# Matmuls ordered by PSUM bank, layer two moved by one chunk, and a new order on VectorE, in a one-core graph layer

## The reference

```
h = relu(layernorm(x))
e = concat(h[src], h[dst], edge_attr)        # 400000 x 96
v = relu(e @ W1 + b1) @ W2 + b2              # 96 -> 64 -> 32
out = x + maximum(segment_max(v, dst), h)
```

## Time and profile before

| | us |
|---|---|
| median of 3 runs | 3184.88 |
| lowest and highest run | 3180.12 and 3187.65 |
| span of the profiled execution | 4798.8 |

### The profile page before, as it was taken

The page is one execution under the profiler, slowest core; times in us unless marked ns, Lnnn a source line. Parts: engine busy times, 40 slices in busy tenths (PEclk is TensorE's granted clock), DMA queues, the critical chain, the costliest instruction groups (busy, mean ns, idle before and its releaser), DMA issues.

```text
span 4798.8 us, 56874 instructions
## 1 busy us (share of the span) xinstructions
PE 3796.5 (79%) x19778; PEld 2547.3 (53%) x19778; DVE 2178.1 (45%) x2474; ACT 2192.4 (46%) x2555; POOL 2386.6 (50%) x2523
## 2 busy tenths in 40 slices
PE   5858788778878877877887788778877887778787
PEld 3536455555555545555555555555555555555465
DVE  4211554445444444544444455444444454445356
ACT  2214454445444444544444445444544454445355
POOL 6653455555455455455545555555455555554310
PEclk8979888888778888888887888888888888888798
DMA  8700222222222222222222222222222222222112
GB/s 255 279 10 25 70 80 88 92 85 61 57 68 63 56 66 69 56 61 68 68 55 63 68 65 61 60 69 68 56 63 68 69 61 56 68 68 68 46 55 56
DMA packets 200553, 350.32 MB, mean 73 GB/s; under 512 B 73791, under 2 KB 124251, under 8 KB 200117
## 3 DMA queue, kind: packets, MB, share of 16 engines
q1 hardware_dynamic: 116638, 303.65, 18.4%
q0 software_dynamic: 80448, 41.33, 6.2%
q10 hardware_dynamic: 3332, 4.01, 0.3%
HBM read 240.36 MB, written 119.78 MB: 75 GB/s over the span
## 4 chain that ended last, share of the span: by engine, by line
PE 60%; issue 19%; another core or an unknown queue 10%; DVE 8%; ACT 2%; DMA 0%; DVEq 0%; ACTq 0%; SPq 0%
PE ps_rows L938 38%; PE ps_layers L968 8%; PE ps_layers L963 5%; DVE onehot L1250 3%; PE ps_layers L918 2%; PE ps_layers L953 2%; PE ps_layers L912 2%; DVE max_t L1318 2%; PE ps_layers L957 2%; PE ps_layers L1006 1%; DVE src_t L1285 1%; DVE rows_in L1323 1%; ACT onehot L852 0%; DVE dst_t L1305 0%
## 5 line engine op out<-in xcount | busy, mean ns | idle before, releaser
L664 POOL DMA_INDIRECT src_in<-h_dram,src_ix x2269 | 2147.7, 947 | 1951.5 <-PE ps_rows L938 976.5
L938 PE MATMUL ps_rows<-onehot,table 128*128 128x512 f32 x9898 | 2553.2, 418 | 109.0 <-issue 89.3
L938 PEld LDWEIGHTS ps_rows<-onehot,table 128*128 128x128 f32 x9898 | 1986.6, 203 | 728.8 <-issue 292.8
L852 ACT ACTIVATE onehot<-distance 128x1024 fp32r<-128x1024 bf16 x909 | 905.0, 1049 | 855.0 <-PE ps_rows L938 607.3
L847 ACT ACTIVATE distance<-picks,below_column 128x1024 bf16<-128x1024 int16 x909 | 985.1, 1139 | 0.7 <-DMA picks<-picks_dram 0.7
L838 ACT ACTIVATE hid<-ps_layers,b_col 128x512 f32<-128x512 f32 (+1 forms) x404 | 241.6, 680 | 1407.9 <-remote 912.0
L1300 DVE STREAM_TRANSPOSE ps_layers<-rows_in 128x512 f32<-128x512 f32 x202 | 133.3, 706 | 1561.3 <-ACT hid L838 1561.2
L968 PE MATMUL ps_layers<-picked_rows,w_src 128*64 128x128 f32 x1552 | 399.9, 390 | 550.1 <-issue 545.7
L1250 DVE SCALAR_TENSOR_TENSOR onehot<-picks,column,ps_layers 128x1024 fp32r<-128x1024 int16 x404 | 499.8, 1258 | 310.2 <-PE ps_rows L938 164.7
L968 PEld LDWEIGHTS ps_layers<-picked_rows,w_src 128*64 128x64 f32 x1552 | 188.8, 180 | 784.9 <-issue 782.2
L1318 DVE TENSOR_TENSOR_SCAN max_t<-mask_in,max_t,ps_layers 128x512 f32<-128x512 bf16 x196 | 249.0, 1271 | 337.2 <-remote 331.4
(11 more groups left out here) (145 smaller groups left out, 1283.1 us busy)
## 6 DMA issues: line engine op xcount, KB each, us to landing
picks<-picks_dram SPq DMA_DIRECT2D x101, 512.0 KB
first_rows<-hid SPq DMA_DIRECT2D x100, 500.0 KB
rows_in<-in_edge_attr_dram SPq DMA_DIRECT2D x96, 512.0 KB
rows_in<-first_rows SPq DMA_DIRECT2D x96, 512.0 KB
run_max<-rows_in SPq DMA_DIRECT2D x96, 512.0 KB
src_in<-h_dram,src_ix POOLq DMA_INDIRECT x2269
mask_in<-mask_dram SPq DMA_DIRECT2D x96, 256.0 KB
h_dram<-h_sb ACTq DMA_DIRECT2D x4, 392.0 KB, 5.9
```

The costliest lines, as they stand in the source:

```text
L664: pool.indirect_dma_start(out=src_in[:, slot, g, r, :], out_offset=None, in_=rows[:, :], in_offset=bass.IndirectOffsetOnAxis(ap=src_ix[:, ...
L852: nc.scalar.activation(onehot[:, RING_AT[c] + BY_DVE[c] + k, :, :].rearrange("p g w -> p (g w)"), distance[:, k, :], ACT.Relu, bias=1.0, s ...
L938: mm = nc.tensor.matmul(ps_rows[g][side][:, 0:WIDE], table[:, i * SIDES + side, part, :], onehot[:, RING_AT[c] + t, g, :], start=(i + part ...
```

## The change

1. `look_up` goes bank by bank. Before, each tile was multiplied into all four banks in turn; now a chunk's tiles all go into bank (side 1, g 0), then (1, 1), (0, 0) and (0, 1). The number of matmuls stays. A counter `banks_summed` tells that a bank is complete in the last chunk; the three tiles of the last chunk are counted together at its end, and in the others `tiles_used` rises at the end of a bank. Chunk 0 waits for the masks of each bank by itself.
2. `mask_rows` starts on each bank when that bank is summed.
3. Layer two stands behind chunk 1 of the look-up instead of behind chunk 0.
4. VectorE's order in a pair becomes: one-hot 0, `mask_rows`, `turn_edges`, `turn_src`, then a wait for the ReLUs of pair j, one-hot 2, `fill_dst`, `find_side`, one-hot 3, `find_max`.
5. Layer one is cut into four functions that TensorE still runs one after the other.

```diff
+BANKS = [(1, 0), (1, 1), (0, 0), (0, 1)]
...
-            def look_up(j, slot, c):
-                if c == 0:
-                    wait(pe, rows_masked, j * MASKS)
-                if BY_DVE[c]:
+            def look_up_bank(j, c, n):
+                side, g = BANKS[n]
+                if c == 0 and (not isinstance(j, int) or j > 0):
+                    if side:
+                        pe.wait_ge(second_side, j * 2 - 1 + g)
+                    else:
+                        pe.wait_ge(rows_masked, j * MASKS - 1 + g)
+                if n == 0 and BY_DVE[c]:
                     pe.wait_ge(onehot_made, j * DVE_ALL + (DVE_AT[c] + 1))
                 for t in range(CHUNK[c]):
...
+                    for part in range(parts):
+                        mm = nc.tensor.matmul(ps_rows[g][side][:, 0:WIDE], table[:, i * SIDES + side, part, :],
+                                              onehot[:, RING_AT[c] + t, g, :],
+                                              start=(i + part == 0), stop=(i == last_tile and part == parts - 1))
+                if c == CHUNKS - 1:
+                    if n < len(BANKS) - 1:
+                        mm.then_inc(banks_summed, 1)
+                    else:
+                        mm.then_inc(tiles_used, CHUNK[c])
+                elif n >= len(BANKS) - CHUNK[c]:
                     mm.then_inc(tiles_used, 1)
...
-                look_up(j + 2, slot, 0)
+                    look_up(j + 2, 0)
+                look_up(j + 2, 1)
                 if mini:
                     layer_two_mini(j, ps_v)
                 else:
                     layer_two(j)
-                for c in range(1, CHUNKS):
-                    look_up(j + 2, slot, c)
+                for c in range(2, CHUNKS):
+                    look_up(j + 2, c)
...
             def mask_rows(j, slot):
                 wait(dve, hid_summed, j * A - A)
-                dve.wait_ge(tiles_used, j * TILES + WIDE_TILES)
                 for g in range(2):
+                    dve.wait_ge(banks_summed, j * (len(BANKS) - 1) + (g + 1))
...
                 turn_edges(j + 1, 1 - slot, of_next * D + D)
+                turn_src(j + 1, (k + 1) % (2 * AHEAD), turn + (k + 1) // (2 * AHEAD))
+                dve.wait_ge(hid_made, j * A + A)
+                dve.sem_inc(layer_passed, 1)
+                one_hot(j + 2, slot, 2)
                 fill_dst(j + 1, 1 - slot, of_next * D + D, of_next * D + D, j + 1)
-                one_hot(j + 2, slot, 2)
+                find_side(j + 2, slot)
+                one_hot(j + 2, slot, 3)
                 find_max(j, slot, stored)
-                one_hot(j + 2, slot, 3)
-                find_side(j + 2, slot)
-                turn_src(j + 1, (k + 1) % (2 * AHEAD), turn + (k + 1) // (2 * AHEAD))
```

More of the change, by code:

```diff
@@ L928, in look_up @@
                     pe.wait_ge(onehot_made, j * DVE_ALL + (DVE_AT[c] + 1))
                 for t in range(CHUNK[c]):
-                    if t == BY_DVE[c]:
+                    i = CHUNK_AT[c] + t
+                    if n == 0 and t == BY_DVE[c]:
                         pe.wait_ge(act_onehot_made, j * ACT_ALL + (ACT_AT[c] + BY_ACT[c]))
[L932 to L940, removed]
+                    if side and i >= WIDE_TILES:
+                        continue
@@ L941, in look_up, with layer_edges @@
                     mm.then_inc(tiles_used, 1)
-            def layer_one(j, slot, ahead=True, short=False):
+            def look_up(j, c):
+                for n in range(len(BANKS)):
+                    look_up_bank(j, c, n)
+            def layer_edges(j, slot):
                 wait(pe, max_scanned, j * 2)
-                pe.wait_ge(onehot_made, j * DVE_ALL + (2 * DVE_ALL + 1 if ahead else (PAIRS - j) * DVE_ALL))
-                pe.wait_ge(side_found, j + 2 if ahead else PAIRS)
-                pe.wait_ge(dst_filled, j * 2 + 2 if ahead else PAIRS * 2)
+                pe.wait_ge(onehot_made, j * DVE_ALL + (2 * DVE_ALL + 1))
+                pe.wait_ge(side_found, j + 2)
+                pe.wait_ge(dst_filled, j * 2 + 2)
@@ L1291, in turn_edges, with fill_dst @@
                     V.transpose(of_half(ea_t[:, slot, :, :], h), ea_in[:, slot, h, :, :]).then_inc(ea_turned, 1)
-            def fill_dst(j, slot, loaded, masks, through, columns=(BLK, BLK), before=(BLK, BLK)):
+            def fill_dst(j, slot, loaded, masks, through, columns=(BLK, BLK), before=(BLK, BLK), made=True):
                 dve.wait_ge(first_loaded[slot], loaded)
@@ L1410, in _ @@
             turn_edges(0, 0, D)
-            fill_dst(0, 0, D, D, 0)
+            fill_dst(0, 0, D, D, 0, made=False)
             def pair(j, k, turn, stored, before_last=False):
@@ L1443, in tail_pair @@
                     dve.wait_ge(side_found, PAIRS)
-                    fill_dst(j + 2, slot, moved_up_to(j + 2), ((j + 2) // 2 + 1) * D, j + 1, columns_of(j + 2), columns_of(j + 1))
-                if j + 1 <= SHORT_AT:
-                    turn_src(j + 1, (j + 1) % (2 * AHEAD), (j + 1) // (2 * AHEAD), j + 1 == SHORT_AT)
+                    fill_dst(j + 2, slot, moved_up_to(j + 2), ((j + 2) // 2 + 1) * D, j + 1, columns_of(j + 2), columns_of(j + 1), made=False)
             for k in range(2 * AHEAD):
```

37 lines of the change are left out of this document (29 added, 8 removed).

## The result

The changed kernel takes 3196.84 us (median of 6 runs, 3194.6 to 3198.22); the kernel before, on the same chip, 3185.25 us (6 runs). The ratio is 1.0035, with an interval of 1.0024 to 1.0047: slower by 11 us, where I had forecast 2 us more and half the chance on no change.

A forecast was written before the change was run, and what follows sets the result against it. POOL's issues were taken to bound the kernel (sum 3173 us, TensorE's 3092). All terms were 0 except 2 us for the shift at the end, added to the median 3184.88: 3187 us, range 3165 to 3224 (own range 3178 to 3198).

The forecast's parts named there:

- What bounds the kernel: Timed kernel bound by POOL's issues: 30.0 us a pair against TensorE's 27.28, last gather at 3040 us, sum 3173 us.
- TensorE's sum: TensorE alone: layer one of pair 0 at 358, 96 pairs of 27.28 us, then 115.5 us: 3092 us.
- Bank order: Look-up matmuls no longer alternating between banks: taken as 0, at most 2.1 us a pair either way.
- earlier one-hots: TensorE needs ScalarE's one-hots sooner in the look-up: cost 0; without the cover 1.4 to 2.8 us a pair.
- layer two at 0: Layer two behind chunk 1, at about 17.7 us of a pair instead of 11.06; its result still precedes find_max.
- Sources turned early: Five steps, 12.6 us, queue behind turn_src; paid once at the end, 0 to a few us, upper bound 12.6.
- 12.5 us to spare: At the end, all pairs stored at G + 101.3 us, before POOL reaches its last seven gathers at G + 113.8.
- POOL's own waits: Ring slots refilled after turn_src, now sooner: gain 0, some 9 us if the opening is 10 us slower; tile signals 0.
- the last chunk's three counts: The last chunk's tile signals come together, up to 2.3 us late, for gathers seven pairs ahead: cost 0.
- Late signals: Rival: VectorE hears late of layer two, delay d = 2.4 us; 0.33 us more a pair, 3217 us; chance 0.17.
- The faster case: Rival: POOL waits for the ring at the opening, 3176 us, or TensorE has uncovered pauses, 3155 us; chance 0.16.
- the clock: Rival: pauses between banks put look-ups at half clock, 3687 us; chance 0.03 together with a bank-order loss.

The follow-up runs named there:

- f1: Bank order of the look-up and bank-wise masks alone, put into the kernel before: 3180.40 us, ratio 0.9996.
- e1: The changed kernel with turn_src put back to the end of VectorE's pair everywhere: 3187.76 us, ratio 1.0018.
- g3: The kernel before with POOL's tile wait relaxed from 6 to 20 and pair 0's turn_src ahead of the first masks: 3180.28 us, ratio 0.9996.
- e3: The changed kernel with turn_src put back to the end in the last pairs (84 to 95) only: 3180.76 us, ratio 0.9996.
- g1: The changed kernel with turn_src just ahead of find_max in the tail pairs alone: 3183.43 us, ratio 1.0003.
- repaired opening and tail: The changed kernel with turn_src last in tail pairs, tile wait 20 instead of 6, pair 0's turn_src ahead of the first masks: 3169.70 us, ratio 0.9961.

## Why the prediction was right or wrong

By its own sign, a move of more than 6 us, the prediction was wrong, though the time lies in its range.

One sum fits all 13 traces. G less POOL's waits is 3027.7 to 3031.7 us in every one, and span − G is 134 to 137 us where the tail turns its sources late, and 145 to 148 where early. The time is POOL's stream, its waits in the opening, and one of two ends.

**What bounds the kernel: right.** The stalls were not in the timed runs (3179.4 us, profiled again), POOL's stream sets the time, and TensorE, at 27.27 us a pair from pair 13 on, meets it late. G came out at 3040 us against 3042.3, but by two errors that cancel. The stream is shorter than I took it (scatters end at 340 us and not 344, and a gather takes (3042.30 − 358.24 − 2.7)/2148 = 1.248 us after the first wait, 6 us less over 2155), and 13.1 us of waits, which I had not seen, fill the gap.

TensorE's sum was too short. Layer one of pair 96 comes at 3064.8 us in before and not at 358 + 2619 = 2977. Of the 88 us, 7 are the later start, 36 the first 14 pairs (29.8 us each), and 45 waits in later pairs, 20 of them in pair 82:

```profile
2668.89 0.33 SPq L453 DMA_DIRECT2D src_ix<-in_src_dram  x1
...
2672.95 0.57 SPq L476 DMA_DIRECT2D mask_in<-mask_dram  x1
...
2679.75 1.32 DVE L1300 STREAM_TRANSPOSE ps_layers<-rows_in 128x512 f32<-128x512 f32 x2 [20.43 <-DMA mask_in<-mask_dram]
```

In the kernel's code SyncE loads new indices only when the gathers of the ring's last slot have landed, and the mask that `fill_dst` needs stands behind that load. Pair 82 lasts 43.9 to 47.2 us in all 13 traces, and layer one of pair 83 comes 340.2 to 340.9 us ahead of G in each, even where the loop's pairs take 27.55 us. So there TensorE falls into step with POOL again, and what an edit does to span − G it does in the 14 pairs from 83 on.

**Bank order, earlier one-hots, layer two at 0: right**, by the runs with bank order alone and with layer two put back. VectorE's chain was forecast at 15.0 us with a margin of 1.1 us; it takes 2014.92 − 2000.23 = 14.7 us with a margin of 1.42.

**Sources turned early: the failed step.** The mechanism was right, and so was the length of the queue behind `turn_src`, from the turning to layer one: 12.6 us forecast, 15.8 − 3.4 = 12.4 us measured (10.0 at pair 95: its gathers had landed 3.7 us sooner than those of pair 94 before, and in before TensorE gained 1.3 us on POOL from pair 94 to 95). Wrong was "12.5 us to spare". I put the last pair's layer one 5.3 us behind the last gather. In the kernel before it comes at 3064.8, 22.5 us behind it, for two reasons. The short pair 96 takes POOL 13 gathers, while TensorE needs its full 27.3 us from the layer one of pair 95: from the last gather of pair 94, POOL has 46.2 us to go and TensorE, from that pair's layer one, 55.9. And that layer one comes 3008.85 − 2996.07 = 12.8 us behind the gather, not 5.3: its last gather is turned 9.3 us after its issue, where I had used 1.2 from the scatter rows. (In the changed kernel, where VectorE waits for them, it is 4.9 to 5.3 us in pairs 89 to 94; why pair 94 before takes longer is open.) So POOL already waited 3.42 us before the change. There was nothing to spare, and the shift was paid in full: about 10 us, near the upper bound of 12.6, where I took 2.

**POOL's own waits: both terms mis-sized.** I took the ring wait at 0 in the likeliest case; it was there in before, 13.1 us. I had asked only about the slot of pair 1. POOL first stands 11.05 us at the slot of pair 0, since that `turn_src` is done at 357.3 us, 18 us after the scatters. The change doesn't move it, and this wait is 5.3 to 9.3 us in the other traces whose opening isn't repaired. At the slot of pair 1, 2.06 us are left then; this wait is there in each run of before's order of sources (1.92 us in f1, 5.12 in e1, 11.39 in g3) and in none with early sources. So what the change itself gives back is some 2 us, and 11 only when the first slot is free. 7.2 us of tile waits, which I had also put at 0, outweigh it.

These waits are for the first tile of chunk 0 and not, as I had priced, for the last chunk's three counts. The tile comes late because layer one is late in the opening (pair 13 begins at 761.4 us, before at 753.2). Their size varies: e3 and g1 open with the same code as the changed kernel and have 4.7 and 9.8 us of them. The cause of the slower opening stays open. It goes with the new order of the one-hots, `fill_dst` and `find_max` together with layer two's place. Bank order and early sources are ruled out; putting layer two back alone or `find_max` half-way back alone didn't end it, and `fill_dst` behind the one-hot of chunk 2 wasn't tried by itself. The last section has a lead.

**The rivals.** Late signals of d = 2.4 us would have made pairs of 27.28 + 2.4 − 1.1 = 28.6 us, and they last 27.27. The faster case had its lever, the ring, but the change pulls it only in part; repaired opening and tail bring 3169.7 us, under the 3176 of its first price. As to the clock, the look-up runs at 0.234 us in bank order, TensorE is busy 400.00 of 400 us from 2000 to 2400 us at a granted clock of 1.00, and over the longer window it is 0.98 where it was 0.99. Pauses between banks, as the Trainium skill ("TensorE: Matmul & The Clock Gate", section "A second HAM failure mode: psum-queue depth-cycling") tells them of another kernel, don't show here.

## What to carry to other kernels

Where one engine's stream feeds a pipeline, a step that waits for that stream should stand last on its engine in the pairs that drain it, and early in the pairs that fill the ring: here the same line of code cost 10 to 12 us at the end, and in the opening it gave some 2 us by itself and 11 us once the slot ahead of it was free too. Before "there is slack at the end" goes into a sum, walk the last two work items through every engine, since a short last item doesn't shorten the engines that don't scale with it (pair 96: 13 gathers instead of 24, but TensorE's pair 95 in front of it is a full 27.3 us). A wait removed at one slot of a ring is a gain only when the next slot is free in time as well.

## What the runs showed that I had not expected

A load's landing time depends on where in the run it is. The DMA view of before, profiled again, first between 440 and 780 us, then between 1200 and 1600 (the last number is the median from issue to landing):

```profile
picks<-picks_dram SPq DMA_DIRECT2D x11, 512.0 KB, 25.1
...
run_max<-in_edge_attr_dram SPq DMA_DIRECT2D x1, 848.0 KB
...
picks<-picks_dram SPq DMA_DIRECT2D x14, 512.0 KB, 10.9
```

In the chain that ended last of the changed kernel these loads stand in 11 pairs of the opening, beginning so:

```profile
421.98 26.48 DMA picks<-picks_dram
453.62 25.07 DMA picks<-picks_dram
```

The load goes out when `mask_rows` is done; 25 us of landing, a one-hot of 2.5 and masks of 2.7 make a round of some 30 us, which is about what the pairs of the opening last in all these traces. In that stretch SyncE's queue also fills an array from `edge_attr`, and later it doesn't. That the fills make the load slow is argued from these rows, and wasn't tried.

They can't be all of it. From 1200 to 1600 us, without fills, the same load lands like this in the run with layer two back behind chunk 0:

```profile
picks<-picks_dram SPq DMA_DIRECT2D x14, 512.0 KB, 18.3
```

There SyncE issues it 7.1 us behind the load of the mask (median), in before 14.8 us: with `find_max` last on VectorE the mask, the store and two more loads of 512 KB go out closer ahead of it. In the opening the two distances are 9.2 us after and 15.1 before, and in the chains that ended last the load takes 25.9 us on average after (11 loads) and 25.0 before (9). Some 0.9 us in each of 11 rounds would be 10 us, and pair 13 is 8 us late. It is a lead and not shown: no run moves `find_max` alone all the way back.
